# A one-column exponential on ScalarE ahead of the leads of self and cross attention

## The reference

```
# first block
hs  = attention(x @ Wq, ctx[:, :-4] @ Wk, ctx[:, :-4] @ Wv, heads=8)
ca  = two small attentions of the last four context tokens
x   = (hs + ca) @ Wout + b_out + x
# second block
h1  = layernorm(x);  x = attention(h1 @ q1, h1 @ k1, h1 @ v1, heads=20) @ o1_w + o1_b + x     # "self"
h2  = layernorm(x);  x = attention(h2 @ q2, ctx @ k2, ctx @ v2, heads=20) @ o2_w + o2_b + x   # "cross"
h3  = layernorm(x);  a, g = split(h3 @ ff_w1 + ff_b1)
x   = (a * gelu(g)) @ ff_w2 + ff_b2 + x
```

## Time and profile before

| | |
|---|---|
| median of 3 runs | 874.06 us (873.12 to 874.97) |
| span of the profiled execution | 871.2 us; the profile gives no other total for it |
| TensorE (PE) matmul, busy | 809.5 us, 93% |
| VectorE (DVE), busy | 596.4 us, 68% |
| ScalarE (ACT), busy | 474.1 us, 54% |
| GpSimd (POOL), busy | 119.5 us, 14% |
| mean granted clock of TensorE | 0.963 of full speed |

### The profile page before, as it was taken

The page is one execution under the profiler, slowest core; times in us unless marked ns, Lnnn a source line. Parts: engine busy times, 40 slices in busy tenths (PEclk is TensorE's granted clock), DMA queues, the critical chain, the costliest instruction groups (busy, mean ns, idle before and its releaser), DMA issues.

```text
span 871.2 us, 11443 instructions
## 1 busy us (share of the span) xinstructions
PE 809.5 (93%) x4148; PEld 443.6 (51%) x4148; DVE 596.4 (68%) x1068; ACT 474.1 (54%) x720; POOL 119.5 (14%) x197
## 2 busy tenths in 40 slices
PE   5999999999999998999989659999999999899998
PEld 3777644444466665333326323333333333678888
DVE  4455576777675557799947587999999971784231
ACT  4643454445544533576687225777667778863130
POOL 4100104100005332000014400000000000540000
PEclk9999999999999998799999857999999999999999
DMA  8886578523310174122134500222232000600000
GB/s 294 269 283 199 153 224 271 132 70 88 100 40 32 68 253 112 39 75 74 39 73 74 194 1 20 48 52 51 56 56 56 2 2 1 257 0 1 31 1 31
DMA packets 30966, 83.18 MB, mean 95 GB/s; under 512 B 5172, under 2 KB 9212, under 8 KB 28606
## 3 DMA queue, kind: packets, MB, share of 16 engines
q1 hardware_dynamic: 30110, 79.71, 31.9%
q0 software_dynamic: 800, 2.73, 0.9%
HBM read 56.12 MB, written 25.89 MB: 94 GB/s over the span
## 4 chain that ended last, share of the span: by engine, by line
PE 65%; DVE 15%; DMA 9%; ACT 5%; issue 4%; SPq 2%; POOL 0%; ACTq 0%; DVEq 0%; POOLq 0%
PE PS L975 19%; PE PS L918 14%; PE PS L1570 8%; PE PS L955 7%; PE PS L619 6%; DVE maxp L1097 5%; DMA k_d<-split 4%; PE PS L1588 4%; DVE negm L1097 3%; PE PS L1389 2%; DMA q_sl<-msplit 2%; ACT probs L1057 2%; DVE maxp L1111 2%; DVE turned L1143 1%; DMA w_raw<-in_ff_w 1%
## 5 line engine op out<-in xcount | busy, mean ns | idle before, releaser
L1057 ACT ACTIVATE probs<-PS 128x1024 f32<-128x1024 f32 (+1 forms) x336 | 310.4, 971 | 139.9 <-PE PS L955 137.0
L1097 DVE TENSOR_REDUCE maxp<-PS 128x1 f32<-128x512 f32 (+1 forms) x400 | 251.6, 678 | 43.4 <-PE PS L918 42.4
L918 PE MATMUL PS<-k_sl,q_sl 48*128 48x512 f32 (+2 forms) x592 | 225.5, 455 | 10.0 <-DVE maxp L1097 2.0
L955 PE MATMUL PS<-q_sl,k_sl 50*128 50x512 f32 (+3 forms) x672 | 203.9, 435 | 9.9 <-ACT probs L1057 6.0
L918 PEld LDWEIGHTS PS<-k_sl,q_sl 48*128 48x128 f32 (+2 forms) x592 | 103.5, 190 | 168.0 <-DVE maxp L1097 105.8
L1097 DVE TENSOR_REDUCE negm<-PS 128x1 f32<-128x512 f32 (+1 forms) x192 | 121.5, 677 | 27.7 <-PE PS L918 27.1
L955 PEld LDWEIGHTS PS<-q_sl,k_sl 50*128 50x128 f32 (+2 forms) x672 | 102.8, 192 | 56.8 <-ACT probs L1057 25.4
L975 PE MATMUL PS<-probs,v2c 128*32 128x512 f32 x640 | 88.1, 620 | 1.0
L661 DVE TENSOR_TENSOR split<-PS,split 128x512 fp32r<-128x512 f32 (+3 forms) x54 | 34.9, 649 | 54.8 <-ACT split L636 54.6
L975 PE MATMUL PS<-probs,v0c 128*64 128x512 f32 (+1 forms) x256 | 62.0, 605 | 0.0
L636 ACT CAST split<-PS 128x512 fp32r<-128x512 f32 (+3 forms) x54 | 29.9, 554 | 53.5 <-PE PS L619 38.8
(11 more groups left out here) (186 smaller groups left out, 1072.6 us busy)
## 6 DMA issues: line engine op xcount, KB each, us to landing
k_d<-split SPq DMA_DIRECT2D x20, 512.0 KB, 3.9
q_d<-split SPq DMA_DIRECT2D x12, 512.0 KB, 4.0
k_sl<-k_d SPq DMA_DIRECT2D x8, 640.0 KB
k_sl<-k_d SPq DMA_DIRECT2D x40, 128.0 KB
q_sl<-q_d SPq DMA_DIRECT2D x40, 128.0 KB
k_sl<-k_d SPq DMA_DIRECT2D x20, 256.0 KB
w_raw<-in_ff_w SPq DMA_DIRECT2D x1, 3840.0 KB, 11.6
k_sl<-k_d SPq DMA_DIRECT2D x8, 320.0 KB
```

The source lines that it names most:

```text
L918: nc.tensor.matmul(PS[0:a.qt, SBANKS[k % 3], 0:cn], q_view(g)[f:f + a.rows, j // a.stack, q * a.qt:(q + 1) * a.qt], k_view(g)[f:f + a.rows ...
L955: mm = nc.tensor.matmul(PS[0:sz, 2 * (x % 2) + half, 0:a.nq], k_view(g)[f:f + a.rows + 2, j // a.stack, t * 128:t * 128 + sz], q_view(g)[f ...
L1057: nc.scalar.activation(probs[0:a.size[t], x % PRING, :, 0:a.nq], PS[0:a.size[t], 2 * (x % 2):2 * (x % 2) + 2, 0:a.nq], ACT.Exp, scale=a.sc ...
L1097: nc.vector.tensor_reduce((maxp if nch > 1 else negm)[0:a.qt, g.turn, o:o + 1], PS[0:a.qt, SBANKS[k % 3], 0:a.chunks[c][1]], AX.X, ALU.max ...
```

## The change

A tile `warm` of one column is added. ScalarE writes into it the exponential of `eps`, once behind join0 and the wait for `v1_set`, and once behind join1. No instruction reads `warm`. Nothing else is changed; the tiles placed behind `warm` move by 32 bytes.

```diff
--- before.py
+++ after.py
@@ -254,6 +254,7 @@
     rstd = place("rstd", [128, TT])
     std = place("std", [128, TT])
     eps = place("eps", [128, 1])
+    warm = place("warm", [128, 1])
     ca_raw = place("ca_raw", [128, 2, 8 * KF])
     kbd = place("kbd", [128, B, KF, H0, NCA])
     vbd = place("vbd", [128, B, KF, H0, NCA], offset=r1 + 31744)
@@ -1719,10 +1720,12 @@
             act_ca_tail(act)
             act_join(act, join0, self_in, selfp)
             act.wait_ge(v1_set, 1)
+            nc.scalar.activation(warm[:, :], eps[:, :], ACT.Exp)
             act_attention(act, S_SELF, side=self_side)
             act.wait_ge(loaded_q2, 16)
             cross_in.act(act, "wq2")
             act_join(act, join1, cross_in, crossp)
+            nc.scalar.activation(warm[:, :], eps[:, :], ACT.Exp)
             act_attention(act, S_CROSS)
             act_join(act, join2, ff_in)
             act_ff(act)
```

## The result

| | before | changed |
|---|---|---|
| median of 22 runs | 872.24 us (867.38 to 877.46) | 866.53 us (861.42 to 873.48) |
| ratio, 95% interval | | 0.9937 (0.9918 to 0.9956) |
| span of the profiled execution | 871.2 us | 867.5 us |
| forecast | | 871.5 us (869.4 to 873.6) |

Two later measurements of the same kernel gave 0.9953 (0.9925 to 0.9982) and 0.9964 (0.9946 to 0.9982). The mean over all of its 46 runs is 867.9 us with a standard error of 0.4. The kernel before has a mean of 871.8 with 0.2 over the 183 runs made beside these measurements and those of the experiments; two more, of 880.9 and 883.1 us at a lower mean clock, are left out of this mean as slow ones. The difference is 3.9 us with a standard error of 0.4, and that is the figure to be explained.

The account below looks back on a forecast made before the run. TensorE bounds the chain (65%) and stands still for two exponential table loads on ScalarE. 874.06 us less 2.59 (1.30 self, 1.29 cross attention), with 0 for added work and nothing from the clock, gave 871.5, range 869.4 to 873.6.

Parts of the forecast that it names:

- The placement of the loads: Leads of both attentions: table loads move to the added exponentials, near 310.0 and 490.5; casts and copies need none.
- The cover: Both leads: added load and exponential cost 0; self attention's next cast 0.27 us late, absorbed; cross attention has 20.73 idle.
- Rival 4: Self attention's lead: late cast lengthens TensorE's wait, clock falls there, 12.3 us more, 883.8; chance 0.04 with any other loss.
- The sum's two terms: Starts of self and cross attention: loads leave the chain, saving 1.30 and 1.29 us, 2.59 in all.
- What is late next: Both starts: VectorE's maxima do not hold TensorE; in cross attention 0.62 us of margin remain, so savings hold in full.
- The base of the forecast: Whole kernel: starting time 874.06 us, the 871.2 span plus 2.86, the median excess of three timed runs.
- The clock: Both attention loops' starts at 1.2 GHz: no gain credited; bound 1.05 us either way at each place.
- I take it that the rise follows the work: Both attention loops: the return to full clock comes 1.3 us earlier too, so the clock adds nothing.
- The prediction's own sign of being wrong: Changed kernel's profile: load stays on chain, VectorE wait replaces the exponential's, or slow-clock stretches change by over 3 us.
- rival 1: Both attention loops: clock rises at the same moments as before; savings worth 0.85 us each, 1.69 in all, 872.4; chance 0.17.
- rival 2: Both attention loops: clock rises earlier than the work; 1.05 us more at each place, 2.1 in all, 869.4; chance 0.09.
- theory G: From the experiments, not the prediction: the clock's share goes up and down with the moment at which the loop starts.

Follow-up runs that it names:

- h4: Kernel before, loads still on the chain, with 128-row matmuls added on TensorE in cross attention alone (lead and second pair's scores); ratio 1.0013 (0.9991 to 1.0036).
- h5: Changed kernel with 128-row matmuls added on TensorE in cross attention alone, two ahead of the second pair's scores; ratio to before 0.9978 (0.9951 to 1.0006).
- h2: Kernel before, loads still on the chain, with 128-row matmuls added on TensorE in the leads of self and cross attention; ratio 1.0007 (0.9984 to 1.0030).

## Why the prediction was right and wrong

**The placement of the loads: right.** The load comes with the first instruction that needs it, so both moved to the new lines, at 310.14 and 487.77. The casts and copies in the leads brought no table back.

**The cover: right.** In self attention the next cast was late by 0.2 us and not 0.27, and TensorE's wait behind it kept its 1.34 us. In cross attention the load lay in idle time of 20 us (it began at 487.77, and the next cast at 508.48). Rival 4 did not come.

**The sum's two terms: right.** 1.28 and 1.28 measured, 1.30 and 1.29 put down. The Trainium skill (ScalarE: Activation LUTs, "What ACT_TABLE_LOAD costs") counts 1.38 us of draining beside each load. That shows neither in the rows nor in the times here: over the 303 runs a load costs 0.0 us (0.1) beyond its pause. The first result, 5.5 us, came near to twice 2.66 through the clock and by chance.

**What is late next: right.** TensorE's product behind VectorE's last wide maximum had no wait at the start of cross attention.

**The base of the forecast: wrong.** "With that, 874.06 less 2.59 = 871.5" starts from three runs. Over 22 runs the median of the kernel before is 872.24, and over 183 the mean is 871.8, with single runs from 865.8 to 877.7. The first step that failed is "runs that scatter by 0.9 to either side of their median": the scatter has a standard deviation of 2.5. That is 1.8 us of the 5.0 between forecast and result. From 872.24 the same sum gives 869.6, and a range as wide as the stated one would begin at 867.5, still above the 866.53 measured. So the base alone does not explain the miss.

**The clock: price right, mechanism wrong, term mis-sized.** The second step that failed is "I take it that the rise follows the work", which set the clock's term at nothing, with 1.05 us at each place as its bound. The rise does not follow the work: in self attention it came 14.8 us behind TensorE's resumption before, and 10.2, 3.7 and 10.0 us behind it in three profiles of the changed kernel. The prediction's own sign of being wrong, slow stretches that change by more than 3 us, came true at once (14.8 to 10.2). Neither rival 1 nor rival 2 is borne out as it stood: the rise keeps no moment, and the low time is no function of the pause. Bounds taken from two stretches of one profile, 3.0 us apart, were too narrow. Eleven us lie between the shortest and the longest. As to the size, the timed runs of the changed kernel have 55.9 us at the low clock, and those of before 59.4 beside the 2.6 us of their longer pauses. These 3.5 us (error 0.8) less are worth 1.3 us at 0.38. With the 2.6 of the loads that is 3.9, the difference measured.

**Luck in the first result.** Its 22 runs have a mean of 866.9, and the two repetitions of the same kernel have 869.1 and 868.7 with medians of 869.24 and 869.41. A surplus over the loads of 3 us, as in the first result, would not have been there in either.

**What stays open.** The kernels differ in their time at the low clock by more than the scatter of their runs explains: 62.3 us behind a stall of 2.3, 53.0 behind one of 4.6. That is what theory G says, but no run shows what decides it. So it is shown that the change is worth 2.6 us by its loads and that the remaining 1.3 us came through the clock. It is not shown that another kernel would get these 1.3 us from the same change. The recorded clock is a mean over the whole run, so it doesn't tell in which stage the low time went.

## What to carry to other kernels

A one-column instruction of the next function, put where ScalarE is idle, takes a table load off the chain for nothing, and what it is worth for certain is the pause that it removes. Where the mean granted clock of each run is on record and the kernels differ only in such pauses, take the low time off before they are compared: here it turned points up to 2.1 us off their line into points within 0.6 of it. Look in the chain for a load that starts only when its input is there. Before a gain of a fraction of a per cent is forecast in an absolute time, count how many runs the base rests on; and where TensorE starts a loop at 1.2 GHz, put down some us of uncertainty for how long it stays there, though the change does not touch it.

## What the hardware showed that was not expected

- The time at the low clock behind the start of self attention's loop was 3.7, 10.0 and 10.2 us in three executions of one kernel.
- A table load cost what its pause cost and nothing beyond it, 0.0 us (0.1), over 303 timed runs of ten kernels.
- With its products of 48 rows doubled, TensorE was busy for 84% of the lead of cross attention (18.43 of 21.90 us) at a granted clock of 0.50. With products of 128 rows between them it was busy for 81% (22.04 of 27.10 us) and the clock was 1.00 in the profile of h4; in that of h5, with the same products, it was 0.50 from 508.9 to 512.3 all the same. Holding the clock there did not pay: the timed runs of h4 have 34.7 us at the low clock and those of h2 24.7, where the kernel before has 62.0, and yet their means are 873.5 and 872.4 us.
- One-column exponentials in a row cost ScalarE 0.10 us each (36 in 3.39 us), though a single one is recorded with 0.20.
